# Attention denominators over four key tiles at a time: half the ones-matmuls, accumulating transfers from GpSimd's queue, six probability buffers

## What is computed

```python
q, k = rope(layernorm(x)), rope(ctx)                 # 16 heads of width 32
scores = jnp.einsum('bqhd,bkhd->bhqk', q, k) * scale + bias[None]
attn = jax.nn.softmax(scores, axis=-1)
out = jnp.einsum('bhqk,bkhd->bqhd', attn, v)         # v = ctx, no rope
x = x + jnp.tanh(g_xattn[0]) * out
x = x + jnp.tanh(g_ffn[0]) * ffn(layernorm(x))       # 512 -> 1536 -> 512, quantized
```

## Time and profile before

| | us |
|---|---|
| median of three runs (1969.28 to 1972.32) | 1970.21 |
| the profiled execution, its own time | 1968.86 |
| span of its records, first to last instruction | 1967.1 |
| from the first to the last copy of denominators (start of L1058), 31 halves | 915.9 |
| TensorE busy in the span | 1738.3 |
| GpSimd busy in the span | 898.7 |

### The profile page before, as it was taken

How to read it: one execution, slowest core, us unless ns; L and a number is a source line. 1 busy time by engine, 2 the same in 40 slices (tenths; PEclk the granted TensorE clock), 3 DMA queues, 4 the chain that set the end, 5 groups by cost and what they waited for, 6 DMA issues and landing times. The chain is left out here.

```text
span 1967.1 us, 26173 instructions
## 1 busy us (share of the span) xinstructions
PE 1738.3 (88%) x9360; PEld 662.5 (34%) x9360; DVE 1484.7 (75%) x2117; ACT 1187.7 (60%) x1911; POOL 898.7 (46%) x411
## 2 busy tenths in 40 slices
PE   1899999999999999999986999999999910299999
PEld 0222333323333323333223554544444400044444
DVE  6899888888787787887845665648999999855442
ACT  2476776777777777666651232228997678854441
POOL 3499999989999999998630010110000000000000
PEclk9999999999999999999997999999999965599999
DMA  4332233112332222221024565547885357755542
GB/s 113 88 115 81 77 87 87 48 49 57 87 88 55 59 61 82 76 56 25 20 97 133 179 204 201 185 153 245 261 269 194 131 178 248 236 186 170 177 161 75
DMA packets 170914, 250.45 MB, mean 127 GB/s; under 512 B 30272, under 2 KB 101312, under 8 KB 170272
## 3 DMA queue, kind: packets, MB, share of 16 engines
q1 hardware_dynamic: 170784, 248.78, 40.2%
HBM read 146.74 MB, written 76.68 MB: 114 GB/s over the span
## 5 line engine op out<-in xcount | busy, mean ns | idle before, releaser
L1024 ACT ACTIVATE P<-quad 128x512 f32<-128x512 f32 x1024 | 557.1, 599 | 243.3 <-PE quad L852 242.9
L1205 DVE TENSOR_REDUCE cm<-quad 128x1 f16<-128x1024 f32 x512 | 601.0, 1216 | 116.5 <-PE quad L839 116.3
L1718 POOL TENSOR_TENSOR Ps<-P,P 128x2048 f32<-128x2048 f32 x124 | 563.0, 4540 | 85.5 <-ACT P L1024 85.3
L852 PE MATMUL quad<-QA,KA 101*128 101x512 f16 x1024 | 352.9, 385 | 6.3 <-ACT P L1024 5.2
L984 PE MATMUL quad<-Wd,oh 128*128 128x512 f16 x768 | 231.6, 382 | 129.5 <-DVE ol L1558 129.5
L839 PE MATMUL quad<-KA,QA 100*128 100x512 f16 x1024 | 323.4, 390 | 24.1 <-issue 7.4
L888 PE MATMUL quad<-P,cg 128*32 128x512 f32 x2048 | 272.7, 604 | 3.6 <-ACT numT L1052 0.6
L1098 ACT ACTIVATE ev<-quad 128x1024 f32<-128x1024 f32 x96 | 97.4, 1015 | 209.6 <-PE quad L945 204.9
L1441 DVE TENSOR_REDUCE mxt<-ev 128x1 f32<-128x1024 f32 x96 | 116.8, 1217 | 113.3 <-ACT ev L1098 113.3
L852 PEld LDWEIGHTS quad<-QA,KA 101*128 101x128 f16 x1024 | 84.2, 97 | 344.8 <-ACT P L1024 233.9
L945 PE MATMUL quad<-x_hi,Wg 128*128 128x512 f16 x768 | 189.2, 381 | 3.6 <-DVE x_lo L1437 3.6
(11 more groups left out here) (143 smaller groups left out, 2095.7 us busy)
## 6 DMA issues: line engine op xcount, KB each, us to landing
gate_scratch<-ev SPq DMA_DIRECT2D x48, 512.0 KB, 2.9
gt<-gate_scratch SPq DMA_DIRECT2D x48, 512.0 KB, 5.6
up_scratch<-ev SPq DMA_DIRECT2D x48, 512.0 KB, 3.1
uf<-up_scratch SPq DMA_DIRECT2D x48, 512.0 KB, 4.9
uf<-up_scratch SPq DMA_DIRECT2D x96, 256.0 KB, 3.6
wt_scratch<-wh SPq DMA_DIRECT2D x72, 128.0 KB, 2.6
cg<-in_ctx_dram SPq DMA_DIRECT2D x16, 512.0 KB, 3.8
xl<-in_x_dram SPq DMA_DIRECT2D x32, 256.0 KB, 4.4
```

The costliest lines, as they stand in the source:

```text
L852: e.matmul(K.score[a], K.KA[k][0:101, a * T + 128 * kt:a * T + 128 * kt + 128], K.QA[k][0:101, T * qc + 512 * a:T * qc + 512 * a + 512], s ...
L1024: e.activation(K.Pb[pb][:, h, :], K.score[h % 2], ACT.Exp, scale=SCALE / (QPOW * KPOW)).then_inc(K.a_exp, 1)
L1205: e.tensor_reduce(cm[:, u:u + 1], K.quad[UNIT["max", hm, u] % 2][:, :], AX.X, ALU.max).then_inc(K.v_max, 1)
L1718: e.tensor_tensor(K.Ps[n % 2][:, :, :], K.Pb[(st.g - 1) % NP][:, :, :], K.Pb[st.g % NP][:, :, :], ALU.add).then_inc(K.g_sum, 1)
```

## The change

In all halves but the last, a sum covers four key tiles. GpSimd adds the first two (tiles 0 and 1 into `Ps[0]`, tiles 4 and 5 into `Ps[1]`). The third and the fourth tile are added to it by transfers from SBUF to SBUF that accumulate in float32, issued from GpSimd's queue, 1 MiB each. The second of them is issued when the first has landed, since both write the same tile. TensorE has two denominator groups in a half, at s = 6 and at s = 2 of the next half. Six probability tiles are used in turn. The copy, the transposes and the residual addition of a half come one step later, and so do the statistics, some loads, and parts of the weight preparation. The last half is as before.

```diff
-NXL, NWL, NWQ, NP = 7, 4, 2, 4
+NXL, NWL, NWQ, NP = 7, 4, 2, 6
...
-        put(110 + 8 * k, "wturn", 0, k)
-        put(114 + 8 * k, "wstore", 0, k)
+        put(115 + 8 * k, "wturn", 0, k)
+        put(118 + 8 * k, "wstore", 0, k)
...
-        self.out = hf - 1 if s == 3 and 1 <= hf <= NHALF else None
+        self.out = hf - 1 if s == (3 if hf == NHALF else 4) and 1 <= hf <= NHALF else None
...
-        self.sum = (hf, s // 2) if self.inside and s % 2 == 1 else None
+        last = hf == NHALF - 1
+        self.sum = (hf, s // 2) if last and s % 2 == 1 else (hf, s // 4) if self.inside and s % 4 == 1 else None
+        self.accumulate = None
+        if s in (2, 4, 6) and self.inside and not last:
+            self.accumulate = (hf, (0, 0, 1)[s // 2 - 1], (2, 3, 6)[s // 2 - 1])
+        elif s == 0 and 1 <= hf < NHALF:
+            self.accumulate = (hf - 1, 1, 7)
...
+        if s == 6 and self.inside and not last:
+            self.dens = (hf, 0)
+        elif s == 2 and 1 <= hf < NHALF:
+            self.dens = (hf - 1, 1)
...
-                e.wait_ge(K.g_sum, 4 * hf + n + 1)
+                e.wait_ge(K.d_acc[n], 32 * hf + 32)
...
-            if m // 2 < 4 * (NHALF - 1):
-                e.wait_ge(K.g_sum, m // 2 + 1)
+            hm, km = m // 8, m % 8
+            if hm < NHALF - 1 and km % 4 < 2:
+                e.wait_ge(K.g_sum, 2 * hm + km // 4 + 1)
+            elif hm < NHALF - 1:
+                e.wait_ge(K.d_acc[km // 4], 32 * hm + 16 * (km % 4 - 1))
...
+        if st.accumulate is not None:
+            hf, n, kt = st.accumulate
+            e.wait_ge(K.a_exp, score_no(hf, kt, 3))
+            if kt % 4 == 2:
+                e.wait_ge(K.g_sum, 2 * hf + n + 1)
+            else:
+                e.wait_ge(K.d_acc[n], 32 * hf + 16)
+            e.dma_start(K.Ps[n][:, :, :], K.Pb[(8 * hf + kt) % NP][:, :, :], accum_op=ALU.add).then_inc(K.d_acc[n], 16)
```

More of the change, by code:

```diff
@@ L69, in gate_weight_jobs @@
         put(100 + 8 * k, "wdivide", 0, k)
-        put(102 + 8 * k, "wround", 0, k)
-        put(103 + 8 * k, "wrounded", 0, k)
-        put(108 + 8 * k, "wscaled", 0, k)
-        put(110 + 8 * k, "wturn", 0, k)
-        put(114 + 8 * k, "wstore", 0, k)
+        put(106 + 8 * k, "wround", 0, k)
+        put(108 + 8 * k, "wrounded", 0, k)
+        put(110 + 8 * k, "wscaled", 0, k)
+        put(115 + 8 * k, "wturn", 0, k)
+        put(118 + 8 * k, "wstore", 0, k)
     return jobs
@@ L98, in other_weight_jobs @@
     return jobs
-NORM_TILES = {9: (0,), 11: (1, 2, 3), 12: (4,), 13: (5, 6), 15: (7,)}
+NORM_TILES = {10: (0, 1), 12: (2, 3, 4), 14: (5, 6), 15: (7,)}
 class Step:
@@ L133, in __init__ @@
             self.rope = (1, (g + 10) // 3, (g + 10) % 3)
-        self.add = hf - 1 if s == 4 and 1 <= hf < NHALF else None
+        self.add = hf - 1 if s == 5 and 1 <= hf < NHALF else None
         self.norm = []
@@ L142, in __init__ @@
         self.load_context = p + 2 if w == 1 and 1 <= p and p + 2 < NQ else None
-        self.load_columns = p + 3 if w == 5 and 0 <= p and p + 3 < NQ else None
+        self.load_columns = p + 3 if w == 6 and 0 <= p and p + 3 < NQ else None
         self.stack = (p + 1, w - 1) if 0 <= p and 1 <= w <= 4 and p + 1 < NQ else None
         self.rows = self.hm if 0 <= self.hm < NHALF and self.im == 7 else None
-        self.store = p - 1 if w == 6 and 1 <= p <= NQ else None
-        self.sum = (hf, s // 2) if self.inside and s % 2 == 1 else None
-        self.dens = None
-        if s % 2 == 1:
-            h, n = (hf, s // 2 - 1) if s > 1 else (hf - 1, 3)
-            if 0 <= h < NHALF:
-                self.dens = (h, n)
+        self.store = p - 1 if w == 7 and 1 <= p <= NQ else None
+        last = hf == NHALF - 1
[5 more added lines that the diff above has]
+            self.accumulate = (hf - 1, 1, 7)
+        self.dens = None
+        if s == 6 and self.inside and not last:
+            self.dens = (hf, 0)
+        elif s == 2 and 1 <= hf < NHALF:
+            self.dens = (hf - 1, 1)
+        elif last and s in (3, 5, 7):
+            self.dens = (hf, s // 2 - 1)
+        elif hf == NHALF and s == 1:
+            self.dens = (hf - 1, 3)
         self.num_out = hf - 1 if s == 1 and 1 <= hf <= NHALF else None
-        self.den_out = hf - 1 if s == 2 and 1 <= hf <= NHALF else None
+        self.den_out = hf - 1 if s == (2 if hf == NHALF else 3) and 1 <= hf <= NHALF else None
         self.stats = None
-        if w >= 13 and 0 <= p < NQ:
-            self.stats = (p, 0, w - 13)
-        elif 5 <= w < 8 and 1 <= p <= NQ:
+        if w >= 14 and 0 <= p < NQ:
+            self.stats = (p, 0, w - 14)
+        elif w == 0 and 1 <= p <= NQ:
+            self.stats = (p - 1, 0, 2)
+        elif p == NQ and 5 <= w < 8:
             self.stats = (p - 1, 1, w - 5)
+        elif 6 <= w < 9 and 1 <= p < NQ:
+            self.stats = (p - 1, 1, w - 6)
         self.aggregate = self.deviation = None
@@ L231, in max_no, with den_no @@
     return 16 * hm + u + 1
+def den_no(hf, n):
+    return 2 * hf + n + 1
 def rope_no(p, w):
@@ L409, in __init__ @@
         self.d_x2s = sem("d_x2s")
+        self.d_acc = [sem(f"d_acc{i}") for i in range(2)]
         self.d_wl = [sem(f"d_wl{i}") for i in range(NWL)]
@@ L912, in tensor_program @@
             else:
-                e.wait_ge(K.g_sum, 4 * hf + n + 1)
+                e.wait_ge(K.d_acc[n], 32 * hf + 32)
             for h in range(4):
-                mm = e.matmul(K.den[32 * h:32 * h + 32, :], K.ones[:, :], K.Ps[n % 2][:, h, :], start=n == 0, stop=n == 3)
+                mm = e.matmul(K.den[32 * h:32 * h + 32, :], K.ones[:, :], K.Ps[n % 2][:, h, :], start=n == 0, stop=n == (3 if hf == NHALF - 1 else 1))
             mm.then_inc(K.pe_den, 1)
@@ L1054, in scalar_program @@
             hf = st.den_out
-            e.wait_ge(K.pe_den, 4 * hf + 4)
+            e.wait_ge(K.pe_den, den_no(hf, 3 if hf == NHALF - 1 else 1))
             if hf > 0:
@@ L1376, in vector_program @@
             e.wait_ge(K.a_exp, score_no(st.hf, st.s, 3))
-            e.wait_ge(K.pe_den, 4 * st.hf + n - 1)
+            e.wait_ge(K.pe_den, den_no(st.hf - 1, n) if n < 2 else den_no(st.hf, n - 2))
             e.tensor_tensor(K.Ps[n % 2][:, :, :], K.Pb[(st.g - 1) % NP][:, :, :], K.Pb[st.g % NP][:, :, :], ALU.add).then_inc(K.v_sum, 1)
@@ L1713, in gpsimd_program @@
             hf, n = st.sum
-            k = 4 * hf + n
             e.wait_ge(K.a_exp, score_no(hf, st.s, 3))
-            if k >= 2:
-                e.wait_ge(K.pe_den, k - 1)
-            e.tensor_tensor(K.Ps[n % 2][:, :, :], K.Pb[(st.g - 1) % NP][:, :, :], K.Pb[st.g % NP][:, :, :], ALU.add).then_inc(K.g_sum, 1)
+            if hf > 0:
+                e.wait_ge(K.pe_den, den_no(hf - 1, n))
+            e.tensor_tensor(K.Ps[n][:, :, :], K.Pb[(st.g - 1) % NP][:, :, :], K.Pb[st.g % NP][:, :, :], ALU.add).then_inc(K.g_sum, 1)
+        if st.accumulate is not None:
[6 more added lines that the diff above has]
+            e.dma_start(K.Ps[n][:, :, :], K.Pb[(8 * hf + kt) % NP][:, :, :], accum_op=ALU.add).then_inc(K.d_acc[n], 16)
     deviation_2(B - 1)
```

## The result

| | before | after |
|---|---|---|
| median, us | 1969.74 (1969.14 to 1972.32, 4 runs) | 2242.55 (2225.93 to 2256.40, 4 runs) |
| ratio | | 1.1379, 95% interval [1.1282, 1.1475] |
| 31 halves, start to start of the denominators' copy | 915.9 | 1185.5 |
| one half | 29.55 | 38.24 |

The change makes the kernel 273 us slower, where I had predicted 42. Nearly all of it lies in the attention: 31 halves have become 269.6 us longer. The profiled execution took 2256.4 us, the upper end of the four.

The account below looks back on a forecast made before the run. TensorE was taken as the bound, GpSimd close behind; with the change, 18.3 us plus two landings (12.6) makes a half 30.9 us, 1.35 more, x 31 = 42 us, so 2012 us; range 1914 to 2085.

Parts of the forecast that it names:

- the chain: Exponentials, GpSimd's sum, two landings in series, TensorE's group, next half's exponentials: no half can be shorter than this.
- the full gain: Two denominator groups fewer in each of 31 halves on TensorE: 54 us, a half of 27.8 us, time 1916.
- faster: The case that transfers land quickly enough for the kernel to gain; chance 0.42.
- The sentence on the six tiles: ScalarE's reuse of six probability tiles adds no wait that the rings don't have; with four it would.
- D: Time from issue to landing of one accumulating transfer: 6.3 us taken, bounds 4.3 and 7.9 us.
- my own ring: The closed loop of waits through one half: 18.3 us weighted plus 2D, 30.9 us as forecast.
- The groups' worth: Each denominator group removed from TensorE gives 0.87 us; 62 of them 54 us.
- GpSimd's busy time: In a half it falls from 26.3 to about 17.2 us, plus four issues.
- Rival 1: Old sum's fetch runs beside the new tile's, landings are quick, kernel faster: 1914 to 1966; chance 0.42.
- Rival 2: GpSimd bounds through issue costs: with 2 us an issue 31.9 us a half, 2043; needs over 1.4 us; chance 0.06.
- Rival 3: VectorE's reduced slack holds TensorE with quick transfers, taking 5 to 15 us off the gain; no separate chance given.
- TensorE's share: TensorE's busy share of the attention stretch falls to about 90%.

Follow-up runs that it names:

- e2: The change with only the first transfer of each pair; tiles 3 and 7 are left out of the denominators: 2018.0 us, ratio 1.024.
- e1: The change without its transfers; tiles 2, 3, 6 and 7 are left out of the denominators: 1924.3 us, ratio 0.977.
- e5: The change with its four transfers sent to two tiles nobody reads, groups waiting only for GpSimd's sums: 2223.4 us, ratio 1.129.
- e14: e5 with the row maxima's transfers issued from ScalarE's queue instead of SyncE's: 2152.9 us, ratio 1.095.
- e8: The change in full, with the row maxima's transfers issued from ScalarE's queue instead of SyncE's: 2214.0 us, ratio 1.125.
- e7: e2 with the row maxima's transfers issued from ScalarE's queue instead of SyncE's: 1941.4 us, ratio 0.986.
- e9: Against the change: GpSimd makes all four two-tile sums, one transfer adds each pair, later groups, row maxima on ScalarE's queue; whole computation: 1994.8 us, ratio 1.013.
- e3: The change with its four transfers copying instead of adding, so denominators are incomplete: 2044.1 us, ratio 1.038.
- e12: Whole computation with one pair transfer and three groups in a half, row maxima on ScalarE's queue: 1974.5 us, ratio 1.004.
- e13: e9 with the residual addition moved from GpSimd to VectorE: 2065.34 us, ratio 1.0489.
- e17: The kernel before with the residual addition moved from GpSimd to VectorE: 1970.95 us, ratio 1.0010.

## Why the prediction was wrong

**The step that failed.** It is the sentence "What counts is not the traffic but the chain that they lengthen." e2 has slack in the chain and is 94 us slower than e1; e5 and e14 have the traffic without the awaited chain, and are 299 and 229 us slower. The chain then adds little: 19 us from e5 to the change, 61 from e14 to e8. The rows for it were in my hands. The transfer engines were at 24% of a half, 7.1 us of 29.55, and I had worked out 2.7 us for one fetch of a MiB: four additions with two fetches are 21.6 us, together 28.7 us of engine time in a half. That is more than the 27.8 us of the full gain, and 93% of the 30.9 of my forecast. The runs confirm the size: the engines' share times the half is 0.73 x 38.24 = 27.9 us in the change, 0.76 x 36.94 = 28.1 in e8 and 0.81 x 34.7 = 28.1 in e14. By this sum the full gain, the far end of my case "faster", was out of reach from the start. The sum doesn't give the measured 38 us by itself: at 73 to 81% the engines are not full, and the rest is transfers that come late.

**What is late then.** SyncE's queue, of which the prediction says only that its stacking shares the engines. It builds the operands of the next group of heads with 28 small issues, and the row maxima that the next score needs stand behind them. Before, they were issued at 515.75 for a score whose exponential starts at 521.01: some 5 us from issue to use, so no view of waits named them. Moved to another queue they give 77 us with two transfers (e2, e7) and 67 (e9), but 29 with four, where the chain and SyncE's other transfers (e14) hold the time as well. The causes don't add up: traffic alone gives most of the loss, and the chain alone, which no run could have without its traffic, would give 163 us by the sum below.

**The sentence on the six tiles** ("the buffers add no wait") stands: no wait of ScalarE for a landing shows.

**The price of D** was mis-sized: 6.3 taken, 8.1 measured in the median and 8.24 in the mean of the 124 landings, above my upper bound of 7.9; the quickest took 6.9. With 8.24 my own ring gives 18.3 + 16.5 = 34.8 us a half, 163 us more than before, some 2132 in all. This slip alone would have put the time above my range (2085), and the other 110 us are what the chain doesn't have. Of these 3.4 us of a half, 1.3 went when the row maxima moved (38.24 to 36.94 in e8); the other 2.1 are not split, and the lower clock after a wait has a part in them (1.2 us in the one ring shown).

**What held.** The groups' worth (45 of 54 us), the ring's form (e8's ring closes, with terms longer than mine), GpSimd's busy time (640.7/31 = 20.7 us, of which four issues of 0.88: 17.1 without them, my 17.2). Rival 1 fell with D, and by e3 would have fallen short with quick landings too. Rival 2 fell: an issue costs 0.88 us, less than 1.4. Rival 3 could not come up. TensorE's share was to be 90% and is 79%.

**Open.** Why an issue on SyncE's queue takes 1.4 to 2 us instead of 0.6 beside these transfers was not tested; that it goes with traffic is shown, by e5. The clock's share of the loss is open too. No arrangement beat the kernel before with the whole computation: the nearest are e12 (1.0035) and e9 (1.0128). e7 (0.986) leaves tiles out.

## What to carry to other kernels

Before adding transfers, add up the transfer engines' time like that of any engine, share of before plus bytes at the measured rate, twice for a transfer that adds; if it comes near the time of the unit, the landing times of the old profile no longer hold. Then look for the transfers that are needed soonest and stand last in a long queue: a wait that the profile doesn't show may be a few us away. Moving work off a full engine helps only if the engine that takes it is not held up by that engine's instructions, as VectorE was in e13.

## What the hardware showed that I had not expected

- An accumulating transfer of 1 MiB from SBUF to SBUF takes 5.35 us of all sixteen engines, a copy 2.80; they land after 8.1 and 5.1 us.
- TensorE's clock falls after a long wait. From 606 us in the change, after a wait of 6.21 us, the granted clock is at half (1.2 of 2.4 GHz) for six us, and the group takes 1.93 us instead of 1.06; then it is back:

```profile
606.00:612.00 6.00, 5.04 (x16) 1.27 (x16) 1.23 (x1) 1.48 (x3) 4.59 (x4) 0.50 0.22 44
612.00:614.00 2.00, 2.00 (x13) 0.56 (x13) 1.82 (x2) 1.56 (x4) 0.64 (x1) 1.00 0.97 197
```

- GpSimd's durations overlap after an issue. In e9 the cosine product is recorded with 2.66 us instead of 2.38, but the next instruction starts 2.33 us after it. The pace is unchanged; spacing of starts tells it, durations don't. The Trainium skill advises the same ("Perfetto Trace Analysis", "GPSIMD Engine Instruction").
- A VectorE addition of two SBUF tiles of 0.68 us took up to 10.8 us beside a GpSimd stream without pauses. Where it was lengthened, in e13 and e17, it ended 0.55 to 0.56 us after a GpSimd instruction did.
